# Linear attention layers: the keys' floor pass moved to GpSimd, two VectorE passes reordered

## What is computed

```python
def _phi(t):
    return jax.nn.elu(t) + 1.0
def layer(h, p):
    q = _phi((h @ wq + bq_).reshape(b, s, H, DH))
    k = _phi((h @ wk + bk_).reshape(b, s, H, DH))
    v = (h @ wv + bv_).reshape(b, s, H, DH)
    kv = jnp.einsum('bshd,bshm->bhdm', k, v)
    z = 1.0 / (jnp.einsum('bshd,bhd->bsh', q, k.sum(axis=1)) + 1e-06)
    att = jnp.einsum('bshd,bhdm,bsh->bshm', q, kv, z).reshape(b, s, d)
    h = _ln(h + att @ wo + bo_, g1_, be1_)
    y = jax.nn.gelu(h @ w1 + c1_, approximate=False) @ w2 + c2_
    return (_ln(h + y, g2_, be2_), None)
```

## Time and profile before

| | us |
|---|---|
| median of 3 runs | 862.58 (862.35 to 863.84) |
| span of the profiled execution | 863.9 |
| time of that execution | 865.69 |
| TensorE busy | 814.1 (94%) |
| VectorE busy | 777.9 (90%) |
| ScalarE busy | 736.0 (85%) |
| GpSimd busy | 407.6 (47%) |

### The profile page before, as it was taken

The page is one execution under the profiler, slowest core; times in us unless marked ns, Lnnn a source line. Parts: engine busy times, 40 slices in busy tenths (PEclk is TensorE's granted clock), DMA queues, the critical chain, the costliest instruction groups (busy, mean ns, idle before and its releaser), DMA issues.

```text
span 863.9 us, 19249 instructions
## 1 busy us (share of the span) xinstructions
PE 814.1 (94%) x5914; PEld 738.6 (85%) x5914; DVE 777.9 (90%) x2675; ACT 736.0 (85%) x1315; POOL 407.6 (47%) x392
## 2 busy tenths in 40 slices
PE   5698999999999999999999999999999999998837
PEld 4588899999999999999999999999999999987624
DVE  6888999989899899989899899989899899998698
ACT  2579899989998899989999899989998899889734
POOL 5233454445544455344544445344544445465482
PEclk9799999999999999999999999999999999999985
DMA  5300200001010100001010100001010000000011
GB/s 147 89 2 2 44 2 18 18 16 30 2 35 2 44 2 22 14 17 28 2 34 2 45 1 24 12 18 27 2 35 2 1 1 2 12 15 1 2 38 61
DMA packets 26264, 18.76 MB, mean 22 GB/s; under 512 B 4354, under 2 KB 22195, under 8 KB 26164
## 3 DMA queue, kind: packets, MB, share of 16 engines
q1 hardware_dynamic: 25300, 16.95, 7.3%
q10 hardware_dynamic: 864, 0.59, 0.2%
HBM read 15.43 MB, written 2.10 MB: 20 GB/s over the span
## 4 chain that ended last, share of the span: by engine, by line
PE 80%; DVE 10%; ACT 7%; issue 3%; DMA 0%; ACTq 0%; DVEq 0%
PE down_ps L764 20%; PE small_ps L697 6%; PE att_ps L727 6%; PE up_ps L754 5%; PE up_ps L756 5%; PE up_ps L755 5%; PE t_ps L675 5%; PE t_ps L734 4%; PE kq_ps L687 3%; PE kq_ps L688 3%; PE kq_ps L689 3%; DVE z_lo L1042 3%; ACT z_hi L915 2%; PE up_ps L718 2%; PE small_ps L705 2%
## 5 line engine op out<-in xcount | busy, mean ns | idle before, releaser
L764 PE MATMUL down_ps<-w_use,hid 128*128 128x128 f32 x2048 | 259.8, 275 | 1.2 <-DVE h L1007 1.0
L764 PEld LDWEIGHTS down_ps<-w_use,hid 128*128 128x128 f32 x2048 | 244.0, 192 | 2.4 <-issue 2.0
L1060 POOL TENSOR_TENSOR res_ffn<-z_tm,g_ffn 128x512 f32<-128x512 f32 x64 | 81.9, 1279 | 249.4 <-DVE k_e L1173 237.9
L1049 POOL TENSOR_TENSOR res_att<-z_tm,g_att 128x512 f32<-128x512 f32 x64 | 82.5, 1288 | 154.4 <-DVE h L1000 154.4
L866 ACT ACTIVATE hid<-up_ps 128x512 f32<-128x512 f32 x192 | 113.3, 592 | 22.3 <-PE up_ps L756 14.8
L1012 DVE BATCH_NORM_STATS2 st<-h 128x6 f32<-128x128 f32 x504 | 107.1, 273 | 0.1
L921 ACT ACTIVATE z_tm<-h,shift,rstd 128x128 f32<-128x128 f32 x244 | 99.9, 483 | 0.0
L754 PE MATMUL up_ps<-z_hi,w_hi 128*128 128x512 f32 x192 | 86.5, 450 | 3.4 <-ACT hid L866 3.4
L1063 POOL TENSOR_TENSOR res_ffn<-res_ffn,ffn_row 128x512 f32<-128x512 f32 x64 | 84.1, 1314 | 5.0
L1052 POOL TENSOR_TENSOR res_att<-res_att,att_row 128x512 f32<-128x512 f32 x64 | 82.3, 1286 | 5.0
L687 PE MATMUL kq_ps<-w_kq_hi,zq_hi 128*128 128x256 f32 x256 | 82.0, 320 | 1.5 <-DVE zq_lo L958 1.5
(11 more groups left out here) (211 smaller groups left out, 2013.7 us busy)
## 6 DMA issues: line engine op xcount, KB each, us to landing
raw_w<-in_L_attn_W SPq DMA_DIRECT2D x15, 256.0 KB, 4.4
out_y<-gate_tm SPq DMA_DIRECT2D x8, 256.0 KB, 2.0
bias_bc<-in_L_attn_c SPq DMA_DIRECT2D x7, 256.0 KB, 4.7
x_tm<-in_L_attn_x SPq DMA_DIRECT2D x3, 512.0 KB, 7.2
raw_rows<-in_L_attn_be SPq DMA_DIRECT2D x15, 64.0 KB, 4.1
raw_g<-in_L_attn_g SPq DMA_DIRECT2D x14, 64.0 KB, 3.1
x_tm<-in_L_attn_x SPq DMA_DIRECT2D x2, 256.0 KB, 3.3
raw_rows<-in_L_attn_bo SPq DMA_DIRECT2D x8, 64.0 KB, 3.8
```

The source lines that it names most:

```text
L764: last = nc.tensor.matmul(down_ps[:, t, :], hid[:, j, t * P:(t + 1) * P], w2_use[:, j, :], start=(j == 0), stop=(j == FC - 1))
```

## The change

The floor pass leaves VectorE. On GpSimd `pool_k_floor` does it as two additions, of minus_one and of ones (a new constant and the old one, 128x128, read again for each of the four tiles), the second waiting for the first. It stands between `pool_res_att` (with the copies of w_v and w_kq, where there are such) and `pool_res_ffn`, and waits for ScalarE's exponential and, from unit 2 on, for z1 of unit u-2. `pool_res_ffn` no longer waits for tk. On VectorE q_elu moves from behind zf to the floor's place, ahead of z1_lo, and k_phi moves behind h2.

```diff
@@ pool_res_ffn
             pool.wait_ge(s["z1n"], TT * (u + 1))
-            pool.wait_ge(s["tk"], min(u + 3, UNITS))
@@ pool_period
             if b == SEQS - 1 and is_layer(l + 1):
                 pool_qk(pool, l + 1)
+            if is_unit(p) and p > 0:
+                pool_k_floor(pool, p)
             if b == 2 and is_unit(p):
@@
-        def dve_k_floor(dve, u):
-            dve.wait_ge(s["kexp"], u + 1)
-            nc.vector.tensor_scalar(k_e[:, :, :], k_e[:, :, :], -1.0, 1.0, ALU.add, ALU.add).then_inc(s["tk"], 1)
+
+        def pool_k_floor(pool, u):
+            pool.wait_ge(s["kexp"], u + 1)
+            if is_unit(u - 2):
+                pool.wait_ge(s["z1n"], TT * (u - 1))
+            nc.gpsimd.tensor_tensor(k_e[:, :, :], k_e[:, :, :], minus_one[:, :].unsqueeze(1).to_broadcast([P, TT, D]), ALU.add).then_inc(s["tk_a"], 1)
+            pool.wait_ge(s["tk_a"], u + 1)
+            nc.gpsimd.tensor_tensor(k_e[:, :, :], k_e[:, :, :], ones[:, :].unsqueeze(1).to_broadcast([P, TT, D]), ALU.add).then_inc(s["tk"], 1)
@@ dve_period
             if proj:
-                dve_k_floor(dve, p + 1)
+                dve_q_elu(dve, p + 1)
             if ln1:
                 dve_z1_lo(dve, p - 1)
             if b == 1 and in_layers(l, 1, L - 1):
                 dve_w1_lo(dve, l)
+            if ffn:
+                dve_h2(dve, p - 2, b)
             if proj:
                 dve_k_phi(dve, p + 1)
-            if ffn:
-                dve_h2(dve, p - 2, b)
             if in_layers(l, 1, L - 2) and b in ZF_TILES and is_unit(p):
                 dve_zf(dve, l, ZF_TILES[b])
-            if proj:
-                dve_q_elu(dve, p + 1)
             if ffn:
                 dve_stats_of(dve, h2[:, b % 2], TT, s["h2_s"], p - 1, "st2_s")
@@ gpsimd, at the start
                 pool_rows(pool, 0)
+                pool_k_floor(pool, 0)
                 pool_att_rows(pool, 0)
```

More of the change, by code:

```diff
@@ L51, in build @@
         ones = sb("ones", [P, P])
+        minus_one = sb("minus_one", [P, D])
         eps_col = sb("eps_col", [P, 1])
@@ L150, in build @@
             row_s qk_ready wv_ready wo_ready gatt_ready gffn_ready w2_ready
-            t2_ps zq_hi_s zq_lo_s kqproj krel kexp tk kphi qrel qexp q_elu_s
+            t2_ps zq_hi_s zq_lo_s kqproj krel kexp tk_a tk kphi qrel qexp q_elu_s
             g_ps_s g_sb_s kv_ps_s blk_s kvo_ps_s kvo_sb q_ks_s den_s den_e_s rden_s qn qn_ps qn_fm
@@ L155, in build @@
             fin_in fin_rows y_a y_s zf_n last_c fin_c out_sent
-            tl_st_s tl_mv_s tl_ln_s tl_r_s tl_mr_s tl_sh_s ew_scaled""".split()
+            tl_st_s tl_mv_s tl_ln_s tl_r_s tl_mr_s tl_sh_s ew_scaled minus_one_s""".split()
         s = {n: sem(n) for n in names}
@@ L1388, in _ @@
                 nc.gpsimd.memset(ones[:, :], 1.0).then_inc(c, 1)
+                nc.gpsimd.memset(minus_one[:, :], -1.0).then_inc(s["minus_one_s"], 1)
                 pool.wait_ge(c, 4)
+                pool.wait_ge(s["minus_one_s"], 1)
                 nc.gpsimd.affine_select(out=ident[:, :], in_=ident[:, :], pattern=[[-1, P]], compare_op=ALU.not_equal,
@@ L1413, in _ @@
                 pool.wait_ge(s["t2m"], 2)
+                pool.wait_ge(s["tk"], 2)
                 nc.gpsimd.memset(e_hid[HID:HID + 1, :, :], 1.0).then_inc(c, 1)
```

## The result

Before: 863.21 us (median of 4 runs, 862.35 to 863.97). After: **890.12 us** (4 runs, 889.72 to 890.65). The ratio is 1.0312, 95% interval 1.0295 to 1.0330. The forecast was 889.6, slower.

What follows compares the result with a forecast made beforehand. TensorE, with 80% of the chain that ended last, was taken as the bound; 6.3 + 12 + 4.5 + 2.8 + 1.9 + 0.5, less 1, is 27.0, on 862.58 gives 889.6 us; range 878 to 897 (0.62).

Steps and rivals of the forecast that it cites:

- (a): Seven periods with w1_lo: GpSimd's second addition holds w1_lo, so k_phi and TensorE's load come 0.90 us later; 6.3 us.
- The 0.5 us for the first layer: First layer: ScalarE has more to do and the queries' exponential for q_elu may come late; 0.5 us in all.
- the gain of 1: VectorE 0.6 us lighter behind k_phi: a gain of at most 1 us, from the few waits for g_sb.
- The sum of 3.08 us: Floor on GpSimd ready 0.13 + 1.68 + 1.27 = 3.08 us after z1; hidden in plain periods, with 0.2 us left.
- my own sign: Plain periods should keep 11.8 us from h1 to h1; if they get shorter, TensorE was not the bound.
- (b): Twelve periods with zf: both zf passes held by res_ffn's passes, g_sb 1.0 us later each; 12 us, least certain.
- (c): Six periods making the next layer's affines: lv held under res_ffn's second pass, 0.75 us each; 4.5 us.
- (d): The start: first k_phi waits for two additions, 1.75 us lost, plus 1.0 for GpSimd's moved list; 2.8 us.
- (e): Last layer, three periods: the floor lengthens GpSimd's list ahead of res_att, which holds den_e; 0.6 us each, 1.9 us.
- Small passes not held twice: Rival: the two zf passes slip through one gap and lv through another; near 873 us, chance 0.20.
- The floor misses the product everywhere: Rival: GpSimd's pair comes 0.5 us later, some 35 plain periods lose 0.3 us each; 900 us, chance 0.10.
- VectorE the pace: Rival: VectorE sets the pace and being lighter pays; 858.6 us, chance of faster 0.04.

Runs made afterwards that it cites:

- five_parts_back: Changed kernel with w1_lo from PSUM, GpSimd waiting for zf, and floors of first two sequences, sequence 4 of each layer and last layer on VectorE: 865.61 us.
- five_back_att_first: five_parts_back with TensorE's attention products moved ahead of the transposes of z1's remainder: 858.33 us.
- w1_from_psum: Changed kernel, but w1_lo reads its first operand from PSUM (k_ps) and not from SBUF (fold_w1): 885.92 us.
- start_on_dve: Changed kernel, but the first two floors stay on VectorE with k_phi directly behind them: 884.59 us.

## Why the prediction was right, point by point

**What bounds it**: right. TensorE's list set the time; VectorE's lighter load bought nothing (five_parts_back, five_back_att_first), and each late handover cost TensorE time.

**Removed and moved**: q_elu fits in the idle time, as said. The moved k_phi costs 0.20 us a layer, in the period with w1_lo alone; that is no further term, since (a) has the 0.60 us of h2 in its sum. The 0.5 us for the first layer and the gain of 1 show in no run apart.

**The floor on GpSimd**: right in size. The sum of 3.08 us from z1 to the floor comes out as 449.36 - 446.28 = 3.08. The first addition is 1.59 us (median of 64), as the one case of the earlier trace rows had it (1.60). Plain periods kept their length where it counts, at TensorE (within 0.04 us). From h1 to h1, as my last paragraph would have it read, some came out shorter (11.75 to 11.19 and 11.27 to 10.84 us), and by my own sign TensorE would then not have been the bound. The sign was ill chosen: h1 only makes up there what it was late before.

**(a), 6.3 us; measured 5.4** (7 x 0.77 in w1_from_psum; against the kernel before the period grew by 0.69, which gives 4.8). From z1's start I had w1_lo's end at 4.74, k_phi at 5.26 and the load at 5.99; the trace has 4.74, 5.26, 5.99. The step that was mis-sized is the last: I set the new load beside the old load. But in the kernel before the load ran ahead of its matmul, whose row is

```profile
437.87 0.83 PE L697 MATMUL small_ps<-k_phi,z_tm 128*128 128x128 f32 x6
```

0.22 us behind the load of 437.65. These 0.22 us are cover, and in the changed kernel load and matmul both start at 451.16. (My last paragraph said "w1_lo still 1.1 us"; by my own sum it had to be 1.64, and was.)

**(b), 12 us; measured 9.4** (6 x 1.56). The double hold is as foreseen, 2.05 us. The same step is mis-sized: the load stood 0.05 us behind g_sb's end in the earlier trace rows, its matmul (452.75) 0.14 behind that; and g_sb came 8.78 us behind z1's start instead of 7.87, 0.9 later and not 1.0. The two periods of a layer grew by 0.74 and 0.87 us.

**(c), 4.5 us; measured 4.1** (6 x 0.68). lv 1.21 us. Right, and the cover of 0.2 was in it.

**(d), 2.8 us; measured 4.6** (start_on_dve; 5.5 by the medians). k_phi came at 17.95 (17.75 foreseen) and its product lost 1.95 us (1.75). What I under-sized is GpSimd's moved list: 1.0 where about 2.6 remain. Its passes hold mr_x (1.25 us, 0.14 before) and den_e (1.28 us, 0.18 before), and q_nt stands behind both: it starts at 29.94 instead of 25.29, 4.65 later. 1.95 and the two holds of 1.1 make 4.2 of that; the upper end I gave, 2.5, was about the value.

**(e), 1.9 us; measured 1.0** (1.7 less the seventh w1_lo; three times 0.6 is 1.8, and I wrote 1.9). The layer is right, the pass for the most part wrong: over half is the hold of lg_e, which I didn't have, and den_e, held before as well, adds 0.6 us at most and not 1.8.

The terms as measured are 5.4 + 9.4 + 4.1 + 4.6 + 1.0 = 24.5, against 27.0. Too large were (a), (b) and (e), too small (d): the forecast met the median to 0.5 us partly because errors cancel. Some of the 26.9 us between the medians I can't place: the layers give 18.3 + 1.7, the start 4.6 to 5.5, and the rest, 1.4 to 2.3 us, is as large as the steps of the start and the tail between profiles of one kernel. The run that was profiled before, 865.7 us, was itself 2.5 above its median.

**Rivals.** Small passes not held twice: out, since the pair takes 2.05 us. The floor misses the product everywhere: out, k_phi waits 5.7 us in all and the plain periods kept their length. VectorE the pace: out, see above. (The lower end of my range, 871, comes to 870 by its own sum: 873.1 less 1.0 and 1.9.)

The Trainium skill (SBUF — State Buffer, Who interferes with whom) has the port pair as an exclusive lock that an instruction with at most one SBUF input, outside some modes, doesn't touch. w1_from_psum agrees, 0.68 against 1.64 us.

## What to carry to other kernels

A pass moved to GpSimd is paid for where its other passes land afterwards: list each short VectorE pass with two SBUF inputs or of tensor_scalar form, however small and however rare, and ask which GpSimd pass lies over it at its new time; a wait put in only moves the hold if GpSimd's next pass then covers another such step. Measure cover at the matmul, not at its weight load. When one engine is full, look for a wait in its own order first: moving one TensorE step here gave 0.6%, and relieving VectorE gave nothing.

## What the runs showed of the hardware

What a hold adds doesn't hang on the held pass's size. 8x8 elements (lg_e) took 1.04 us instead of 0.22, 128x4 (lv) 1.21 instead of 0.15, a full 128x512 pass (w1_lo) 1.64 instead of 0.68: each ended 0.03 to 0.55 us behind the end of GpSimd's pass. With work queued on both sides the two take turns: GpSimd's next pass starts when VectorE's first zf pass ends, and the second zf pass ends 0.08 us behind it, in all twelve periods. And it goes the other way too: GpSimd's first addition, issued while q_nt with its two SBUF inputs is running, takes 1.59 us by the median of 64; in the two cases at the start where q_nt wasn't running it takes 1.26.
